# Two early classes of source blocks in a graph kernel's second gather, and half of its one-hots on ScalarE

## The reference

```python
z = concat([x[src], x[dst], edge_attr]) @ W.T + b          # 106250 x 256
z = (z - mean(z)) * rsqrt(var(z) + 1e-5) * gamma + beta    # over all edges
x1 = layernorm(x + (x + zeros.at[src].add(sigmoid(z[:, :H]) * softplus(z[:, H:]))))
mean_in = segment_sum(x1[src], dst) / max(count(dst), 1)
d = tanh(norm(x1 - mean_in))
h = x1 + 0.2 * (relu(x1 @ W1 + b1) @ W2 + b2) * d
y = layernorm(x1 + layernorm(h) * gamma1 + beta1)
```

## Time and profile before

| what | us |
|---|---|
| median of 3 runs | 3957.51 |
| lowest and highest | 3954.84, 3958.5 |
| the profiled execution, its own time | 3961.72 |
| its span | 3960.0 |
| busy in the span: PE, DVE, ACT, POOL | 2955.8, 2926.6, 2235.5, 2698.6 |

### The profile page before, as it was taken

The page is one execution under the profiler, slowest core; times in us unless marked ns, Lnnn a source line. Parts: engine busy times, 40 slices in busy tenths (PEclk is TensorE's granted clock), DMA queues, the critical chain, the costliest instruction groups (busy, mean ns, idle before and its releaser), DMA issues. The chain is left out here.

```text
span 3960.0 us, 83005 instructions
## 1 busy us (share of the span) xinstructions
PE 2955.8 (75%) x18072; PEld 2010.7 (51%) x18073; DVE 2926.6 (74%) x7805; ACT 2235.5 (56%) x6119; POOL 2698.6 (68%) x2634
## 2 busy tenths in 40 slices
PE   6764888888888999999999956767773466656542
PEld 2321444444435777777777745656663344434431
DVE  8998898999885455455455438999997588777757
ACT  1422999999985666666666659989995010000003
POOL 3887777777776777777777730038888777777770
PEclk8975999999999999999999987889996688787866
DMA  7333333333335888888888894458775444444342
GB/s 220 113 95 93 101 100 104 97 104 97 104 97 173 263 263 259 263 259 261 264 262 260 262 246 166 186 205 300 298 296 193 127 119 119 118 118 118 110 74 41
DMA packets 328965, 687.63 MB, mean 174 GB/s; under 512 B 54430, under 2 KB 202695, under 8 KB 320679
## 3 DMA queue, kind: packets, MB, share of 16 engines
q0 software_dynamic: 113520, 284.01, 25.5%
q1 hardware_dynamic: 173160, 279.21, 21.9%
q10 hardware_dynamic: 42192, 123.38, 8.3%
HBM read 461.69 MB, written 224.69 MB: 173 GB/s over the span
## 5 line engine op out<-in xcount | busy, mean ns | idle before, releaser
L374 POOL DMA_INDIRECT rec_d<-arena x830 | 891.5, 1074 | 311.0 <-issue 310.1
L860 POOL DMA_INDIRECT arena<-b_tab,arena x880 | 838.4, 953 | 292.4 <-issue 261.8
L1283 POOL DMA_INDIRECT x_sb<-x_tab,arena x608 | 580.4, 955 | 191.1 <-issue 171.4
L774 PE MATMUL psum<-arena 128*128 128x440 f16 x3360 | 678.7, 358 | 37.8 <-ACT arena L468 36.3
L881 DVE TENSOR_TENSOR arena<-psum,arena 128x512 f32<-128x512 f32 x440 | 283.5, 686 | 556.8 <-DMA arena<-b_tab,arena 316.9
L1273 POOL DMA_INDIRECT x_sb<-x_tab,l_idx x272 | 371.0, 1364 | 349.2 <-DMA x_tab<-x_sb 266.6
L971 PE MATMUL psum<-weT,arena 128*128 128x256 f32 x1760 | 547.8, 393 | 56.1 <-DVE arena L881 53.1
L1628 PE MATMUL psum<-arena,x_sb 128*128 128x256 bf16 x1824 | 331.3, 361 | 323.6 <-issue 136.6
L468 ACT ACTIVATE arena<-arena 128x128 f16<-128x128 f16 x1680 | 561.6, 386 | 0.0
L633 DVE TENSOR_SCALAR arena<-iota_t,arena 128x880 f16<-128x880 f16 x840 | 500.7, 661 | 58.2 <-PE psum L774 55.4
L774 PEld LDWEIGHTS psum<-arena 128*128 128x128 f16 x3360 | 324.8, 99 | 386.5 <-issue 62.8
(11 more groups left out here) (260 smaller groups left out, 5486.6 us busy)
## 6 DMA issues: line engine op xcount, KB each, us to landing
z_d<-arena ACTq DMA_DIRECT2D x220, 512.0 KB
arena<-z_d SPq DMA_DIRECT2D x44, 2560.0 KB, 9.7
arena<-rec_d SPq DMA_DIRECT2D x220, 260.0 KB, 3.4
arena<-in_edge_attr SPq DMA_DIRECT2D x83, 640.0 KB
early_d<-x_sb POOLq DMA_DIRECT2D x17, 1536.0 KB, 8.3
arena<-early_d SPq DMA_DIRECT2D x34, 768.0 KB, 4.3
arena<-b_tab,arena POOLq DMA_INDIRECT x880
rec_d<-arena POOLq DMA_INDIRECT x831, 3.4
```

What stands on the lines that cost most here:

```text
L374: nc.gpsimd.indirect_dma_start(rec_rows, bass.IndirectOffsetOnAxis(e_idx[:, s, k:k + 1], 0), e_buf[:, s, k, :], None).then_inc(s_es[s], 16)
L774: last = nc.tensor.matmul(bank(4 + 2 * k + h)[:, 0:HALF], hot_lane[:, s, k, :], hot_tile[:, s, h * HALF:(h + 1) * HALF], start=start, stop ...
L860: nc.gpsimd.indirect_dma_start(bg[:, s, k, :], None, b_tab, bass.IndirectOffsetOnAxis(rec[:, s, k, H:H + 1].bitcast(I32), 0)).then_inc(s_b ...
L1283: nc.gpsimd.indirect_dma_start(ring_slot(s)[:, k, :], None, x1_tab, bass.IndirectOffsetOnAxis(gi[:, s, k:k + 1], 0)).then_inc(s_xe[s], 16)
```

## The change

- The sources fall into three classes: blocks 0 to 8, 9 to 23, and the remaining 25. There are 75 keys, padded to 76, and `HK` is 760. Its counts and ranks take two PSUM banks of half the width each. The list has 912 slots in 114 groups, for 880 in 110.
- The first class is normalised and stored once 160 tiles are added, the second at 420 tiles. DVE stops for it twice and works in pieces of three blocks with three buffers. The seventh piece waits until the first six are stored.
- 19 groups of the first class and 33 of the second are gathered early: 52 groups for 34. They are held back less: eight gathers per 12 tiles of messages, for four gathers per eight.
- The order of the last stage is early and direct in turn, 52 times, and ten direct groups at the end.
- DVE makes the one-hots of tiles 0 to 3 of a turn, and ACT those of tiles 4 to 7: relu(1 - (iota - dst) ** 2), in four squares and one Relu of 1024 columns. PE waits for them before tile 4.
- An added store blanks the extra rows of `x1_tab` at the start.

The core of the diff:

```diff
-N_GROUPS = SLOTS // G
-HALF = SLOTS // 2
+ID_COLS = 8
...
-TILE_RUN = 80
-EARLY, EARLY_BLOCKS, EARLY_TILES = 34, 16, 300
-X1_STORED = 16 * (1 + 4)
+TILE_RUN = 76
+CLASS_BLOCKS = (9, 24)
+CLASS_TILES = (160, 420)
+CLASS_GROUPS = (19, 52)
+EARLY, EARLY_BLOCKS = CLASS_GROUPS[-1], CLASS_BLOCKS[-1]
+PIECE = 3
+PIECES = (3, 5)
+X1_EARLY = 16 * sum(PIECES)
+X1_STORED = X1_EARLY + 16 * 4
+assert PIECES[0] * PIECE == CLASS_BLOCKS[0] and sum(PIECES) * PIECE == CLASS_BLOCKS[1]
 PAIRS = -(-BLOCKS // 2)
-KEYS = 2 * PAIRS
+USED_KEYS = 3 * PAIRS
+KEYS = USED_KEYS + USED_KEYS % 2
+LIST_SLOTS = -(-((N_EDGES + KEYS * (P - 1)) // P) // (2 * G)) * (2 * G)
+N_GROUPS = LIST_SLOTS // G
+HALF = LIST_SLOTS // 2
+assert LIST_SLOTS <= ID_COLS * P and LIST_SLOTS % TILE_RUN == 0 and HALF <= 512
...
+                early_rows = x1_tab[ROWS:, :].rearrange("(p b) f -> p (b f)", p=P)
+                sp.dma_start(early_rows, pad_rows[:, 0:EARLY_BLOCKS * ROW // 2].bitcast(BF16)).then_inc(s_blank, 16)
...
-                    after(nc.vector.tensor_reduce(total[:, 0:n], by_col(counted), op=ALU.add, axis=AX_X))
+                    each = n // len(counted)
+                    for i, region in enumerate(counted):
+                        after(nc.vector.tensor_reduce(total[:, i * each:(i + 1) * each], by_col(region), op=ALU.add, axis=AX_X))
...
+                def sources_early_enough():
+                    for i in range(2):
+                        after(nc.vector.tensor_scalar(early_src[:, i:i + 1], tend[:, CLASS_BLOCKS[i] - 1:CLASS_BLOCKS[i]], float(CLASS_TILES[i]), None, ALU.is_le))
                 def early_enough():
-                    after(nc.vector.tensor_scalar(early_key, tend[:, PAIRS - 1:PAIRS], float(G * EARLY), None, ALU.is_ge))
+                    for i in range(2):
+                        after(nc.vector.tensor_scalar(early_key[:, i:i + 1], tend[:, (i + 1) * PAIRS - 1:(i + 1) * PAIRS], float(G * CLASS_GROUPS[i]), None, ALU.is_ge))
                     after(nc.vector.tensor_tensor(early_src, early_src, early_key, ALU.mult))
+                    after(nc.vector.tensor_tensor(early_src[:, 1:2], early_src[:, 1:2], early_src[:, 0:1], ALU.mult))
...
-                after(nc.vector.tensor_scalar(v_a, src_i, float(EARLY_BLOCKS * P), float(PAIRS), ALU.is_ge, ALU.mult))
+                after(nc.vector.tensor_scalar(v_a, src_i, float(CLASS_BLOCKS[0] * P), float(PAIRS), ALU.is_ge, ALU.mult))
+                after(nc.vector.tensor_scalar(v_b, src_i, float(CLASS_BLOCKS[1] * P), float(PAIRS), ALU.is_ge, ALU.mult))
+                after(nc.vector.tensor_tensor(v_a, v_a, v_b, ALU.add))
...
-                    nc.vector.tensor_reduce(pos_d, by_col(bank(0)[:, 0:HK]).rearrange("p b c -> p c b"), op=ALU.max, axis=AX_X).then_inc(s_card, 1)
+                    nc.vector.tensor_reduce(pos_d, psum[:, 0:2, 0:HH].rearrange("p k (b c) -> p c k b", c=G_IN), op=ALU.max, axis=mybir.AxisListType.XY).then_inc(s_card, 1)
...
-                    nc.tensor.matmul(COUNT_D, onesb, hot_c[:, b % 2, :], start=(b == 0), stop=(b == NB - 1)).then_inc(s_cd, 1)
+                    for i, region in enumerate(COUNT_D):
+                        last = nc.tensor.matmul(region, onesb, hot_c[:, b % 2, i * HH:(i + 1) * HH], start=(b == 0), stop=(b == NB - 1))
+                    last.then_inc(s_cd, 1)
...
-                    ranks(bank(0)[:, 0:HK], hot_d, upto_d)
-                    before(bank(0)[:, 0:HK], run_d).then_inc(s_rgd, 1)
+                    for i in range(2):
+                        ranks(bank(i)[:, 0:HH], hot_d[:, i * HH:(i + 1) * HH], upto_d[:, i * HH:(i + 1) * HH])
+                        last = before(bank(i)[:, 0:HH], run_d[:, i * KEYS // 2:(i + 1) * KEYS // 2])
+                    last.then_inc(s_rgd, 1)
...
+        CLASS_CHUNKS = [tiles // (CG * YG) for tiles in CLASS_TILES]
+        assert all(tiles % (CG * YG) == 0 for tiles in CLASS_TILES)
+        def chunks(eng, step, pauses=()):
+            c = 0
+            for stop, pause in [*pauses, (CHUNKS, None)]:
+                while c < stop and (c < CS or c % CS):
+                    step(c, c % CS, c // CS)
+                    c += 1
+                whole = (stop - c) // CS
+                if whole:
+                    with eng.Fori(c // CS, c // CS + whole) as it:
+                        for j in range(CS):
+                            step(CS * it + j, j, it)
+                    c += whole * CS
+                while c < stop:
+                    step(c, c % CS, c // CS)
+                    c += 1
+                if pause is not None:
+                    pause()
...
+        BY_ACT_FROM = 4
+        assert 4 * HEAD >= 2 * len(CH) + 1 and EARLY % 4 == 0 and DIRECT >= EARLY
+        def sum_bank(place, k):
+            return bank((8 * place + k) % RING)[:, 0:Z]
+        def tiles_since(place, k):
+            j = 8 * place + k
+            return RING if j >= RING else j + 64 - max(i for i in range(64) if i % RING == j)
...
-                order = (("early", 2 * i, 0, i + 1), ("direct", 4 * i, 0, i + 1), ("direct", 4 * i + 1, 1, i + 1),
-                         ("early", 2 * i + 1, 1, i + 1), ("direct", 4 * i + 2, 2, i + 1), ("direct", 4 * i + 3, 3, i + 1))
-                for place, (kind, n, s, use) in enumerate(order):
-                    step(6 * i + place, place, kind, n, s, use, None if isinstance(i, int) and i == 0 and place == 0 else before)
-                    before = (6 * i + place, place, kind, n)
+                before = (8 * i - 1, 7, "direct", 4 * i - 1)
+                for k in range(4):
+                    for place, kind, s, use in ((2 * k, "early", k % 2, 2 * i + (k // 2 + 1)), (2 * k + 1, "direct", k, i + 1)):
+                        n = 4 * i + k
+                        step(8 * i + place, place, kind, n, s, use, None if isinstance(i, int) and i == 0 and place == 0 else before)
+                        before = (8 * i + place, place, kind, n)
...
+                def store_early(i):
+                    for piece in range(sum(PIECES[:i]), sum(PIECES[:i + 1])):
+                        rows = x1_tab[ROWS + piece * PIECE * P:ROWS + (piece + 1) * PIECE * P, :]
+                        sp.wait_ge(s_x1e, piece + 1)
+                        sp.dma_start(rows.rearrange("(b p) f -> p b f", p=P), x1ep[piece % 3].rearrange("p b k f -> p b (k f)")).then_inc(s_xs, 16)
+                chunks(sp, load, [(CLASS_CHUNKS[i] + CS, lambda i=i: store_early(i)) for i in range(2)])
...
+                    i = 0 if k < CLASS_GROUPS[0] * G else 1
+                    return CLASS_TILES[i] // YG + 2 + 3 * (k - (0, *CLASS_GROUPS)[i] * G) // (2 * BURST)
...
+                    if g in (0, CLASS_GROUPS[0]):
+                        i = 0 if g == 0 else 1
+                        ready = nc.gpsimd.value_load(need[0:1, i:i + 1], min_val=16, max_val=X1_STORED)
+                        pool.wait_ge(s_xs, ready)
+                        settle(pool, s_turn)
...
-                    if s < 2:
-                        wait(pool, s_sg, 24 * (2 * use) + (8 * s - 80))
-                    else:
-                        wait(pool, s_sg, 24 * (2 * use) + (8 * s - 72))
+                    wait(pool, s_sg, 16 * n - 48)
...
+                def hots(u, place, kind, n, s, use, before):
+                    ahead = XS - 1
+                    if kind == "direct" and not (isinstance(n, int) and n + ahead >= DIRECT):
+                        columns(n + ahead, (s + ahead) % XS, use + 1 if s + ahead >= XS else use)
+                    wait(act, s_sg, 8 * u - 8)
+                    wait(act, s_ha, u)
+                    for k in range(BY_ACT_FROM, G):
+                        t = first_tile(kind, n) + k
+                        last = nc.scalar.activation(off_dst[:, k - BY_ACT_FROM, :], iota256b[:], ACT.Square, bias=l1_loc[:, bass.ds(t, 1)], scale=-1.0)
+                    last.then_inc(s_oa, 1)
+                    wait(act, s_oa, u + 1)
+                    nc.scalar.activation(hotg[:, place % 2, BY_ACT_FROM:G, :], off_dst, ACT.Relu, bias=ones[:, 0:1], scale=-1.0).then_inc(s_ha, 1)
+                    if kind == "direct" and isinstance(n, int):
+                        if n % 2 == 1 and n // 2 < len(CH):
+                            relu(n // 2)
+                        if n % 2 == 0 and 1 <= n // 2 <= len(CH):
+                            enhanced(n // 2 - 1)
...
+                    for q in range(PIECES[i]):
+                        piece = sum(PIECES[:i]) + q
+                        if piece == 3 or piece == 6:
+                            dve.wait_ge(s_xs, 16 * piece)
+                        parts = x1ep[piece % 3]
+                        wait(dve, s_x1e, piece)
+                        nc.vector.memset(x1e[:, :, 0:1], 1.0)
+                        for b in range(PIECE):
+                            at = q * PIECE + b
+                            last = nc.vector.tensor_scalar(x1e[:, b, 1:H + 1], agg[:, first + at, :], two[:, at, 0:1], r[:, at:at + 1], ALU.subtract, ALU.mult)
```

(33 more changed lines are left out.)

170 lines of the change are left out of this document (70 added, 100 removed).

## The result

The changed kernel takes **4137.7 us** (median of 4 runs, 4130.6 to 4144.5) where the kernel before takes 3958.0 beside it: a ratio of 1.0454, 95% interval 1.0438 to 1.0469. That is 180 us slower; the forecast was 106 slower, 4064 us, and the measured time lies above its range of 4000 to 4120. The profiled execution took 4144.5 us, with a span of 4142.8.

A forecast was written before the change was run, and what follows sets the result against it. DVE was to replace POOL as bound in the list and last stage. The list's end +52 us and the last stage +54 gave +106: 4068 us from the profiled 3961.7, 4064 against the median; range 4000 to 4120.

The forecast's parts named there:

- the first stage: Counting and ranking before the list: +12 us for wider compares, +5 us for two added passes.
- the list's sum: List stage: wider scan, compare, reduction and one-hots lengthen DVE's block to 10.43 us from 10.0, +35 us over 82 blocks.
- POOL wants 39.3 us per 4 blocks: List stage: 30 scatters per 4 blocks, each 1.005 us plus 0.305 us of issue, taken as unchanged.
- DVE becomes the bound: List stage: DVE's 41.7 us per 4 blocks exceed POOL's 39.3, so DVE sets the pace.
- the small operations: Small DVE operations in a list block, counted within a block's growth of 1.12 us (0.7 to 1.4).
- Rival 2: List keeps its stalls as ScalarE's fills stay bunched: 92 us for 35, 4121 us in all; chance 15%.
- The classes: Two early classes beside the messages: 416 gathers early for 272, first at 2524, direct gathers starting at 3208 for 3098.
- Rival 3: Early gathers beside the messages run at 1.28 us, not 1.75; direct ones start 138 us earlier, 3926 us; chance 5%.
- The last stage: Second gather and sums: alternating turns move the bound from POOL to DVE, ending at 3935 for 3881, +54 us.
- rival 1: Last stage: the chain of adds closes up without one-hots between, 0.6 us a turn, 62 us, 4002 us; chance 13%.
- The 727: First direct gather (3208) to last add (3935): terms 12, 603 (turns of 5.85), 28, 6.5, 60.5 and 17.4 us.
- turn 104: Last stage: the turn that uses direct group 52; after it only direct groups are left, and the ring holds four.

The follow-up runs named there:

- run 1: Changed kernel with the list's one-hots cut into 19 rows of 48 columns instead of 12 of 76: 4113 us, 1.0343 of the kernel before.
- run 2: Kernel before the change with the list's one-hots cut into 10 rows of 88 columns instead of 11 of 80: 4045 us, 1.0166.
- Run 5: run 1's kernel with each add of the last stage taking 128 of its 256 columns: 4040 us beside 3960, one run.
- run 4: run 1's kernel with the second early class closed at group 36 and two direct turns for an early one: 4065 us, 1.0220.
- run 3: run 1's kernel with all eight one-hots of a last-stage turn on VectorE, none on ScalarE: 4123 us, 1.0372.
- run 7: Changed kernel with empty list slots pointing to different rows instead of all to row 0, two operations added: 1.0404 of the kernel before.

## Why the prediction was wrong

The profiled run lost 182.8 us of span: 20 in the first stage, 105 in the list, and about 57 behind it; the forecast had 17, 35 and 54.

- **The failed step is the list's sum**: "One-hots L633 of 912 columns for 880, 5.85 us for ten: 0 or +0.21; 0.15", and with it "POOL wants 39.3 us per 4 blocks", which was 45 (30 scatters at 1.195 + 0.305). The first took the time of a view from its number of columns alone, and the second took POOL's scatter as a constant. Both hang on one thing, the shape of the one-hot's view, and runs 1 and 2 turn it off and on. Of the 77 us of span that the forecast missed (183 for 106; 74 by the medians) 70 lie in the list; some 38 of them are this (949 us from the first one-hot of the list to the last, for run 1's 911).
- "DVE becomes the bound" was false for this kernel and true for run 1, where the block is 10.83 us for 10.43, 0.40 x 84 = 34 us over my 35. So even without the holds the list would have taken 67 us more than before, and the whole 136 us (run 1's 1.0343), not 106. That is the other 32 us of the 70: terms mis-sized, the one-hots by 0.19 and the small operations by 0.22 a block.
- *Rival 2* had nearly the right price for the list (92 us) and the wrong mechanism: ScalarE's fills never stopped POOL.
- **The classes**: right. Gathers went early, the first at 2648.9 (2524 + 126 = 2650), the direct ones began where the sum had them. *Rival 3* fell: the early gathers cost 1.6 us each (416 in 676 us), not 1.28. The rows above show what keeps them from their free pace, DVE's products and sums of two SBUF operands, and the change left these alone.
- **The last stage**: right in its bound, and in its size partly by luck. 3334.4 to 4063.9 is 729.5 us for 727. Run 5 shows the bound, run 4 what lifting it gives, run 3 that *rival 1* was 5 times too large.
- **The 727** stood on three errors that cancel. Turns in the unrolled rounds take mostly 5.43 us instead of 5.85, as the border shrinks: to turn 56 the stage needs 26 us less than the sum had. In the looped rounds a turn in eight takes 9.1 to 9.6 us, since DVE stands still where a round begins: 18 us more to turn 104. And the six last groups, all empty, arrive every 13.2 us instead of 10.06: 95.5 us behind turn 104, where the sum had 84.4. No step of mine had the last two. DVE at such a border:

```profile
3865.98 0.29 DVE L1590 TENSOR_SCALAR arena<-iota256b,l_loc 128x256 bf16<-128x256 bf16 x1 [3.98 <-issue]
```

- The forecast's own bounds are off by a few us: its terms (14 to 83 in the list, 15 either way behind it) add up to 4011 to 4110, not 4015 to 4105.

No version here beats the kernel before on a chip where that takes 3960 us, beyond what can be measured; run 4, at 1.022, is the best with the new classes and a list that holds for any edges.

## What to carry to other kernels

When a kernel's pace is set by GpSimd's indirect DMAs, count the DVE operations beside them by kind: here those with two SBUF inputs, and the 16-bit one-hots with an even count of rows, held a transfer on POOL until they ended. A resized view is a new operation; before pricing it by its columns, look for a row of the same shape, odd or even in its row count. And padding is not free at the end of a gather: point empty slots to different rows.

## What the runs showed of the hardware

- An indirect DMA of 128 rows takes 0.95 to 0.97 us of POOL, or that plus the rest of a DVE operation of the kinds above: 3.81 us beside the product of 2.81, and 7.17 us, the longest, beside a sum of two SBUF operands that lasts 6.68. The 0.15 us is no sharp rule. In the list of the kernel before, of 77 scatters with a scan running at that moment, 63 were held and 14 were not; after the change, 84 of 85 were. One of the 14, where the scan began at 801.82:

```profile
801.70 0.97 POOL L374 DMA_INDIRECT rec_d<-arena  x1 [0.30 <-issue]
```

  The exact moment stays open.
- 1024 transfers of 768 bytes out of one row take 13.2 us, 12.9 ns each, at 59 GB/s and 0.95 of the DMA engines' time; out of different rows they go at 79 GB/s with 0.30 (run 7), as fast as POOL issues them.
- The one-hot over 912 columns takes 456 ns as 12 x 76 and 678 as 19 x 48; over 880, 452 as 10 x 88 and 661 as 11 x 80; over 864, 655 as 9 x 96. With a one-hot running 0.15 us after the scatter's start, 303 of 319, none of 322, 193 of 291, none of 367 and none of 294 scatters took more than 1.00 us, in this order.
- On two of the chips used the same kernels took a third longer, with DVE, ACT and PE standing still together in the loops, some 10 us at a time in the list. The cause is not known.
